# A two-layer gated transformer step on one core: first attention in four row groups, split weights of the block attention kept in DRAM, its mask added on TensorE

## The reference, cut to what matters

```python
x = x + tanh(g_xattn[0]) * first_attention(layernorm(x), ctx)   # 16 heads of 8, features = axis 1 (128), 256 positions
x = x + tanh(g_ffn[0])   * experts(layernorm(x))                # 64 routed experts and a shared one
x = x + tanh(g_xattn[1]) * mlstm(layernorm(x), ctx, ctx)        # gated linear attention
x = x + tanh(g_ffn[1])   * block(layernorm(x))                  # layernorm, causal RoPE attention (16 heads of 128), MoE
# first_attention, per batch b and head h (q, k, v are 1x1 projections of the features, with biases):
#   scores = q_h^T k_h / sqrt(128)    [256, 256], softmax over the keys, times v_h, projection by Wo
# block attention, per batch and head:
#   q, k = rope(h @ wq + bq), rope(h @ wk + bk);  scores = q k^T / sqrt(128), masked above the diagonal
#   softmax, times v, output projection wo
```

## Time and profile before

| | us |
|---|---|
| three runs | 1807.99, 1817.80, 1822.12 (median 1817.8) |
| profiled execution: time | 1817.43 |
| profiled execution: span from first to last instruction | 1816.1 |
| mean granted clock of TensorE | 0.940 of 2.4 GHz |
| busy: TensorE, VectorE, ScalarE, GpSimd | 1606.5, 1259.6, 1019.4, 765.8 |

### The profile page before, as it was taken

The page is one execution under the profiler, slowest core; times in us unless marked ns, Lnnn a source line. Parts: engine busy times, 40 slices in busy tenths (PEclk is TensorE's granted clock), DMA queues, the critical chain, the costliest instruction groups (busy, mean ns, idle before and its releaser), DMA issues.

```text
span 1816.1 us, 30483 instructions
## 1 busy us (share of the span) xinstructions
PE 1606.5 (88%) x10932; PEld 1268.4 (70%) x10932; DVE 1259.6 (69%) x2321; ACT 1019.4 (56%) x2050; POOL 765.8 (42%) x575
## 2 busy tenths in 40 slices
PE   4379999789999999999986964899899999999898
PEld 2135555368888888888872533788787778888687
DVE  6458788378644455444445576999999999999454
ACT  4247777644433335333335653877776877677453
POOL 5200000024435333333330014798798688877000
PEclk9569899899999999999996987999999999999899
DMA  5613232243343333343400002123112111211220
GB/s 155 154 55 83 76 84 61 80 111 105 94 129 106 104 110 102 108 116 102 118 10 6 4 2 92 48 72 103 56 56 68 56 56 56 68 48 30 70 47 24
DMA packets 73349, 137.42 MB, mean 76 GB/s; under 512 B 12824, under 2 KB 41308, under 8 KB 70384
## 3 DMA queue, kind: packets, MB, share of 16 engines
q1 hardware_dynamic: 73200, 135.48, 26.4%
HBM read 125.70 MB, written 8.95 MB: 74 GB/s over the span
## 4 chain that ended last, share of the span: by engine, by line
PE 54%; DVE 19%; issue 9%; DMA 8%; ACT 6%; POOL 2%; SPq 1%; DVEq 0%; ACTq 0%; POOLq 0%
PE bank L67 13%; PE bank L69 13%; PE bank L68 13%; DMA a_qs<-a_mparts 5%; DVE b_straight L1938 3%; DVE b_straight L1892 2%; PE bank L246 2%; PE bank L232 2%; PE bank L204 2%; ACT b_turned L1809 2%; DVE b_peak L1909 2%; POOL e_hidden L944 1%; DVE b_probs L1907 1%; PE bank L1700 1%; PE bank L1732 1%
## 5 line engine op out<-in xcount | busy, mean ns | idle before, releaser
L944 POOL TENSOR_TENSOR e_hidden<-e_gated,e_comb_wide 128x512 f32<-128x512 f32 x132 | 211.0, 1599 | 346.7 <-DVE e_gated L909 331.1
L784 ACT CAST e_hidden_hi<-e_hidden 128x512 fp32r<-128x512 f32 x132 | 82.0, 622 | 320.6 <-POOL e_hidden L944 320.6
L902 DVE TENSOR_TENSOR e_hidden_lo<-e_hidden,e_hidden_hi 128x512 fp32r<-128x512 f32 x132 | 98.2, 744 | 209.8 <-ACT e_hidden_hi L784 209.8
L423 DVE TENSOR_REDUCE a_negmax<-bank 128x2 f32<-128x512 f32 x256 | 165.6, 684 | 64.6 <-PE bank L204 63.3
L69 PE MATMUL bank<-e_x_hi,e_weights_lo 128*128 128x512 f32 (+1 forms) x528 | 209.5, 397 | 0.0
L67 PE MATMUL bank<-e_x_hi,e_weights_hi 128*128 128x512 f32 (+1 forms) x528 | 208.4, 395 | 0.7 <-ACT e_comb_rows L744 0.7
L68 PE MATMUL bank<-e_x_lo,e_weights_hi 128*128 128x512 f32 (+1 forms) x528 | 208.4, 395 | 0.0
L1809 ACT ACTIVATE b_turned<-bank,b_swap_bias 64x512 f32<-64x512 f32 x256 | 174.9, 683 | 17.7 <-PE bank L69 12.9
L1996 POOL TENSOR_TENSOR b_turned<-b_turned,b_rope 128x512 f32<-128x512 f32 x128 | 167.5, 1329 | 5.3 <-ACT b_turned L1809 4.8
L340 ACT ACTIVATE a_exp<-bank 128x512 f32<-128x512 f32 x256 | 142.9, 596 | 42.8 <-PE bank L232 35.4
L69 PE MATMUL bank<-e_weights_hi,e_hidden_lo 128*128 128x256 f32 (+1 forms) x528 | 149.4, 283 | 0.0
(11 more groups left out here) (326 smaller groups left out, 4318.1 us busy)
## 6 DMA issues: line engine op xcount, KB each, us to landing
e_comb_wide<-e_combT SPq DMA_DIRECT2D x130, 256.0 KB, 4.0
e_raw<-in_e_weights SPq DMA_DIRECT2D x64, 384.0 KB, 4.5
b_raw_qk<-in_b_wqk SPq DMA_DIRECT2D x64, 256.0 KB, 2.8
a_qs<-a_q_parts SPq DMA_DIRECT2D x48, 192.0 KB
a_ks<-a_k_parts SPq DMA_DIRECT2D x48, 192.0 KB
b_raw_v<-in_b_wv SPq DMA_DIRECT2D x16, 512.0 KB, 3.8
b_raw_o<-in_b_wo SPq DMA_DIRECT2D x64, 128.0 KB, 2.0
moe_comb_wide<-b_comb_rows SPq DMA_DIRECT2D x16, 256.0 KB, 6.7
```

The lines of the kernel that those rows point to most:

```text
L423: dve.tensor_reduce(m.negmax[b % 2][:, h, :], banks[h % 2][:, :].rearrange("p (q n) -> p q n", q=2), AX.X, ALU.max, negate=True).then_inc( ...
L944: pool.tensor_tensor(m.hidden[i][0:rows, :], m.gated[i][0:rows, :], m.comb_wide[u % E_RING][0:rows, chunk * BANK:(chunk + 1) * BANK], ALU. ...
```

## The change

**First attention.** q and k are split into two fp32r terms (high, low) instead of three bf16 parts. A head has 24 rows of contraction (three products of 8) and two rows for the maximum; the heads are laid out in four groups of 32 partitions (`LANES`), four heads in each. A slot `t` computes two heads: maxima for slot `t`, exponentials for slot `u = t - LEAD` (15), whose matmuls are issued in turns and lie in other row groups. Projections of the pairs of batches 2 to 7 are moved into the loop; only two pairs are projected ahead of it. One reduction takes the maxima of two heads. The maxima are split on GpSimd ahead of the turn, and two DMAs per batch carry them. Stacks are loaded per pair of batches, with a ring of three pairs. The output bias is added ahead by GpSimd, and VectorE reads the projection from the bank.

**Weights of the block attention.** During the first attention, SyncE loads 32 pieces of 512 columns of wqk, wv and wo, GpSimd rounds and subtracts, and SyncE stores both terms in DRAM. The block attention then loads both terms, with two buffers each, and neither VectorE nor GpSimd splits anything there.

**Mask.** The mask is a bf16 matmul of 512 columns with the identity, which opens the accumulation of the scores; the scale is folded into the rotation table of q. VectorE reads only the maxima; ScalarE takes the exponentials from the bank. The next mask matmul waits for the exponentials instead of for the mask addition.

```diff
-TILES = 4
-A_RING = 4
-AHEAD = HEADS + 3 * HEADS // 4
+A_TERMS, MAX_ROWS = 3, 2
+LANE, LANES = 32, 4
+A_SLOTS = HEADS // 2
+A_PAIRS = NB // 2
+A_RING, A_PARTS, A_MAXIMA, A_EXPS = 3, 2, 4, 8
+LEAD = 15
+A_LAST = NB * A_SLOTS
+A_STEPS = A_LAST + LEAD + A_SLOTS
+TURN_AT, SPLIT_EVERY = A_SLOTS + 2, 2 * A_SLOTS
...
+def projection_of(t):
+    i, at = t // SPLIT_EVERY + 2, t % SPLIT_EVERY
+    return ({0: "q", 2: "k", 4: "v"}[at], i) if at in (0, 2, 4) and i < A_PAIRS else None
...
+def heads_of(slot):
+    j = slot % A_SLOTS
+    return [(2 * (j % 2) + side, j // 2) for side in range(2)]
...
 def layer0_sp(k, m, s, ring):
+    def store(i):
+        sp.wait_ge(s.low, 2 * (i + 1))
+        both = lambda n, part: m.parts[i % A_PARTS][:, n, part, :].rearrange("p (j n) -> p j n", j=2)
+        for n, (dst, terms) in enumerate(((k.q_stack, (0, 0, 1)), (k.k_stack, (0, 1, 0)))):
+            for term, part in enumerate(terms):
+                sp.dma_start(dst[2 * i:2 * i + 2, term].rearrange("j p n -> p j n"), both(n, part).bitcast(F32)).then_inc(ring["stored"][i % A_PARTS], DMA)
+
+    def stack(i):
+        r = i % A_RING
+        sp.wait_ge(ring["stored"][i % A_PARTS], 2 * A_TERMS * DMA * (i // A_PARTS + 1))
+        if i < A_RING:
+            sp.wait_ge(s.ones, A_RING)
+        else:
+            sp.wait_ge(s.exp_scores, (i - A_RING + 1) * 2 * HEADS)
+        for src, dst in ((k.q_stack, m.qs), (k.k_stack, m.ks)):
+            for lane in range(LANES):
...
+
+    def max_rows(b):
+        sp.wait_ge(s.max_copied, b + 1)
+        for part in range(MAX_ROWS):
...
...
+    for i in range(2):
+        store(i)
+        stack(i)
+    for t in range(A_STEPS):
+        at, i = t % SPLIT_EVERY, t // SPLIT_EVERY + 2
+        if t % A_SLOTS == TURN_AT % A_SLOTS and TURN_AT <= t < A_LAST + TURN_AT:
+            b = (t - TURN_AT) // A_SLOTS
+            max_rows(b)
+            if b == 0:
+                for u in range(KEPT_SLOTS):
+                    load_kept(u)
+            else:
+                for u in kept_of(b - 1):
+                    store_kept(u)
+                for u in kept_of(b + 1):
+                    load_kept(u)
+        if at == 5 and i < A_PAIRS:
+            store(i)
+        if at == 9 and i < A_PAIRS:
+            stack(i)
...
 def layer0_pe(k, m, s, ring):
+    def scores(t):
+        u = t - LEAD
+        maximum, exponential = t < A_LAST, 0 <= u < A_LAST
+        if exponential:
+            if u % A_SLOTS == 0:
+                b = u // A_SLOTS
+                pe.wait_ge(ring["max_in"][b % A_MAXIMA], MAX_ROWS * DMA * (b // A_MAXIMA + 1))
+            if u:
+                pe.wait_ge(s.exped, 2 * u - 1)
+            exp_pair(u, 0, 0)
+        if maximum:
+            if t % (2 * A_SLOTS) == 0:
+                i = t // (2 * A_SLOTS)
+                pe.wait_ge(ring["stack_in"][i % A_RING], 2 * LANES * DMA * (i // A_RING + 1))
+            freed(("max", t))
+            max_pair(t, 0, 0)
+        if exponential:
+            exp_pair(u, 0, 1).then_inc(s.exp_scores)
+        if maximum:
+            max_pair(t, 1, 0)
+            max_pair(t, 0, 1)
+            max_pair(t, 1, 1).then_inc(s.max_scores)
+        if exponential:
+            if u:
+                pe.wait_ge(s.exped, 2 * u)
+            exp_pair(u, 1, 0)
+            exp_pair(u, 1, 1).then_inc(s.exp_scores)
...
 def layer0_pool(k, m, s, ring):
+        pool.tensor_copy(high, negmax).then_inc(own.tick())
+        pool.wait_ge(own.sem, own.n)
+        pool.tensor_tensor(low, negmax, high.bitcast(F32), ALU.subtract).then_inc(s.max_split)
+        pool.tensor_scalar(k.resid[:, b, :], k.resid[:, b, :], m.late_bias[:, 0:1], None, ALU.add).then_inc(s.biased)
+        for u in kept_of(b):
+            whole, high = kept_places(k, u, (P, KEPT))
+            pool.wait_ge(ring["kept_in"][u % KEPT_SLOTS], DMA * (u // KEPT_SLOTS + 1))
+            pool.tensor_copy(high.bitcast(F32R), whole).then_inc(s.kept_high)
+            pool.wait_ge(s.kept_high, u + 1)
+            pool.tensor_tensor(whole.bitcast(F32R), whole, high, ALU.subtract).then_inc(s.kept_low)
...
 def attention_sp(k, m, w, s, ring, before):
+    def fetch(split, whole, n, fetched):
+        for i in range(2):
+            sp.dma_start(split[n % 2][i][:, :].bitcast(F32), whole[n % whole.shape[0], i]).then_inc(fetched[n % 2], DMA)
...
+        if 2 <= n + 1 < B_STEPS and n >= 1:
+            sp.wait_ge(s.qk_sums, 2 * n)
+            fetch(w.split_qk, k.qk_parts, n + 1, ring["qk_in"])
+        if 2 <= n - 4 < B_STEPS:
+            sp.wait_ge(s.proj_sums, n - 5)
+            fetch(w.split_o, k.o_parts, n - 4, ring["o_in"])
...
 def attention_pe(k, m, w, s, ring, before):
...
     def scores(n):
+        if n:
+            pe.wait_ge(s.exps, n)
+        else:
+            pe.wait_ge(s.constants, 2)
+        pe.matmul(banks[SC][:, :].rearrange("p (b s) -> p b s", b=CHUNK), w.ident_16[:, :], w.mask_16[:, :].unsqueeze(1).to_broadcast([P, CHUNK, S]),
+                  start=True, stop=False, skip_group_check=True)
         pe.wait_ge(s.rotated, 2 * (n + 1))
-        if n:
-            pe.wait_ge(s.masked, n)
...
 def attention_dve(k, m, w, s, ring, before):
...
-    def softmax(n):
-        dve.tensor_tensor(probs[:, :, :], by_batch(banks[SC][:, :]), w.mask[:, :].unsqueeze(1).to_broadcast([P, CHUNK, S]), ALU.add).then_inc(s.masked)
-        dve.tensor_reduce(w.peak[i][:, :], probs[:, :, :], AX.X, ALU.max, negate=True).then_inc(own.tick())
-        dve.tensor_scalar(w.peak_scaled[i][:, :], w.peak[i][:, :], SCALE, None, ALU.mult).then_inc(s.peaked)
+    def peaks(n):
+        dve.wait_ge(s.score_sums, n + 1)
+        dve.tensor_reduce(w.peak[n % 2][:, :], by_batch(banks[SC][:, :]), AX.X, ALU.max, negate=True).then_inc(s.peaked)
```

More of the change, by code:

```diff
@@ L149, in max_rows @@
-    def max_rows(b):
-        sp.wait_ge(s.max_split, b + 1)
-        for part in range(MAX_ROWS):
-            row = TERM_ROWS + part
-            sp.dma_start(m.qs[b % A_RING][row:row + 1, :, :].rearrange("o h (q n) -> o (h q) n", q=2),
-                         m.mparts[b % 2][:, part, :]).then_inc(ring["max_in"][b % A_RING], DMA)
-    for i in range(1, NB // 2 + 1):
-        store_parts(i - 1)
-        if i == 3:
-            stack(0)
-    for b in range(1, A_RING):
-        stack(b)
-    for i in range(AHEAD):
-        if i >= 2 and (i - 2) % HEADS == HEADS - 1:
-            max_rows((i - 2) // HEADS)
@@ L223, in exponentials @@
-    def exponentials(b, h):
-        bank, r, at = banks[2 + h % 2], b % A_RING, b * HEADS + h
-        if h == 0:
-            pe.wait_ge(ring["max_in"][r], MAX_ROWS * DMA * (b // A_RING + 1))
-        if at >= 2:
-            pe.wait_ge(s.exped, at - 1)
-        else:
-            pe.wait_ge(s.v_copied, NB // 2)
-        for kb in range(2):
-            last = pe.matmul(bank[:, kb * POS:(kb + 1) * POS], m.ks[r][0:ROWS, h, kb * P:(kb + 1) * P], m.qs[r][0:ROWS, h, :],
-                             start=True, stop=True)
-        last.then_inc(s.exp_scores)
@@ new lines, in times_v @@
+    def times_v(g):
+        b, h = divmod(g, GROUPS)
+        pe.wait_ge(s.exped, TILES * (g + 1))
+        pe.wait_ge(s.max_copied, min((g + 3) // GROUPS + 1, NB))
+        if g:
+            pe.wait_ge(s.sums_copied, g)
+        else:
+            pe.wait_ge(s.cleared, 1)
+        for kb in range(2):
+            for lane in range(LANES):
+                last = pe.matmul(banks[SUM_BANK][LANE * lane:LANE * lane + HD + 1, 0:POS], m.vaug[:, b, kb, GROUPS * lane + h, :],
+                                 m.expo[(TILES * g + lane) % A_EXPS][:, kb, :], start=kb == 0, stop=kb == 1)
+        last.then_inc(s.weighted)
@@ L343, in times_v @@
[L343 to L369 removed]
+    for i in range(2):
+        for kind in "qk":
+            high(kind, i)
@@ new lines, in layer0_act @@
+    for chunk in range(1, NCHUNK):
+        root(chunk)
+    act.wait_ge(k.gates_in, DMA)
+    act.activation(k.gates[:, :], k.gates[:, :], ACT.Tanh).then_inc(k.gates_ready)
+    for t in range(A_STEPS):
+        u = t - LEAD
+        if t and projection_of(t - 1) and projection_of(t - 1)[0] in "qk":
+            high(*projection_of(t - 1))
+        if 0 <= u < A_LAST:
+            exponentials(u)
+        if t % A_SLOTS == TURN_AT % A_SLOTS and TURN_AT <= t < A_LAST + TURN_AT:
+            max_to_rows((t - TURN_AT) // A_SLOTS)
+        if u % 2 == 0 and 2 <= u < A_LAST + 2:
+            times_v((u - 2) // 2)
+        if u % A_SLOTS == 4 and u >= 12:
+            to_features(u // A_SLOTS - 1)
@@ new lines, in layer0_dve @@
+    norm_start(0)
+    dve.memset(m.vaug[:, :, :, :, HD], 1.0)
+    dve.memset(banks[SUM_BANK][:, :], 0.0).then_inc(s.cleared)
+    norm_end(0)
+    for kind, i in USES[:4]:
+        read(kind, i)
+    for chunk in range(1, NCHUNK):
+        norm_start(chunk)
+        if chunk == 1:
+            for i in range(2):
+                read("v", i)
+    for chunk in range(1, NCHUNK):
+        norm_end(chunk)
+    dve.wait_ge(s.weights_in, 5 * DMA)
```

(15 more changed lines are left out.)

588 lines of the change are left out of this document (245 added, 343 removed).

## The result

The changed kernel takes 1869.2 us (median, 1867.18 to 1874.99) against 1816.02 of the kernel before on the same chip: ratio 1.030, 95% interval 1.025 to 1.035. It is slower; 1786 was predicted. The profiled run took 1867.18 us, its span is 1865.8.

The account below looks back on a forecast made before the run. TensorE was taken to bound the first attention's main part, VectorE and TensorE closely the block attention. First attention 4, block 26 and its start 1 us gained: 1817.4 - 4 - 26 - 1 = 1786.4 us, range 1754 to 1832.

Parts of the forecast that it names:

- Start: First attention's start: first maximum at 37 us, first exponential at 70 instead of 110.93, 41 us gained.
- Five waits: First attention: TensorE waits five times for the maxima's DMA behind stack loads in SyncE's list, 11 us each, 55 in all.
- Slots: First attention's main part: 113 slots with maxima and exponentials at 3.44 us per four heads, 194 us, bounds 181 to 230.
- 2.0 "without a wait": Sign of being wrong, first attention: a slot costs over 2.0 us without a wait.
- a clock of 1.00 between the waits: Sign expected in the first attention: TensorE's granted clock is 1.00 between the five waits.
- the row groups don't run side by side: Rival, first attention: weight loads follow each other, 1.0 us a head, 32 us more, total 1818; chance 0.19.
- The low clock: Rival, first attention's main part: TensorE's clock stays at 0.50, groups cost 5.5 us, 116 us more, total 1902; chance 0.05.
- no overlap with the waits at their upper bound: Slow end of the range: score matmuls in different row groups not overlapping, five waits totalling 75 us; put at 1832.
- End: First attention's last fifteen slots, only exponentials: 27.4 us, unchanged from the kernel before.
- Kept traffic: First attention: 25 MB of added traffic for rounded block attention weights is hidden, cost zero.
- Block attention: Idle time of 46 us, less 15 for the mask matmul and 5 of waits: 26 us gained, bounds 8 and 31.
- The step of 8.1 us: Sign expected in the block attention: steps of 8.1 us; steps staying at 8.8 would prove the prediction wrong.

Follow-up runs that it names:

- Number 1: Changed kernel with the stack loads issued behind the even batch's maxima in SyncE's list (index 14 instead of 9); 1797.51 us, ratio 0.983.
- number 8: Changed kernel with only VectorE's order edited: residual and quotient ahead of the slot's maxima, stack loads unmoved; 1799.26 us, ratio 0.990.
- number 6: Changed kernel with stack loads behind the maxima in SyncE's list, and VectorE's residual, reciprocal and quotient ahead of its maxima; 1734.21 us, ratio 0.953.
- number 3: Changed kernel with stack loads behind the maxima in SyncE's list and only the residual ahead of VectorE's maxima; 1774.31 us, ratio 0.972.
- number 9: Matmul bursts ahead of even batches' first exponentials: on number 8, 96 narrow 1838.91 us, six wide 1816.22; on the changed kernel, six wide 1861.71.
- numbers 7: As number 3, but only 5 of the 32 pieces of block attention weights are loaded, rounded and stored; 1767.97 us, ratio 0.972.
- number 10: Two kernels: number 6 with the mask added by VectorE, 1712.76 us; number 6's first attention without kept weights plus the old block attention, 1763.38 us.
- number 4: First attention of the kernel before with the weight rounding and storing added, block attention of the changed kernel; 1830.38 us, ratio 1.003.

## Why the prediction was wrong

**Start: right.** First maximum at 33.7 us (37), first exponential at 66.25 (70).

**Five waits: right.** 9.6 to 9.8 us each, 48.5 in all, where the prediction has 55, at the batches that it named, though 51 us apart (48 the last) and not 28; a sixth of 6.4 us lies in the start. Number 1 shows their cause, number 8 their price.

**Slots: the step that failed.** Predicted were 113 slots at "0.86 us a head", 194 us, with bounds of 181 and 230. From 66.25 us to the end of the last slot with maxima at 389.4 are 323 us, less 48.5 for the five waits 274.6: 80 too many, 1.21 us a head. That is 2.43 us a slot, 2.09 without the short waits below, past the 2.0 "without a wait" that the prediction itself names as the sign of being wrong; another of its signs, a clock of 1.00 between the waits, fails too. The term had the engines' work nearly right: number 6 takes 204.9 us for the same 113 slots, 0.91 a head, with the clock at 0.97 over them. Where no projections run beside the slots, its turns of the maxima at 201.32, 214.64 and 227.98 are 13.3 us apart, 0.83 a head. Two things were missing. One is a wait: 38 us of TensorE standing behind VectorE's 1.22 us reduction, at up to three places of a batch, where number 6 has 2 left. The prediction costed the reduction as work of VectorE, at 1.37 at most, and never asked what was queued behind it in VectorE's list. The other is the clock. Number 6's 204.9 and 36 us of waits make 241; the 34 us that are left to 274.6 go with the lower clock: 0.72 from 66 us to the end of the first attention, where number 6 has 0.99. So the 80 are 36 of waits, 34 of the clock and 10 by which the slots' own work was costed too low. That the short waits also bring the lower clock is shown by number 6: it takes only 14 us of them out of number 3, its clock over the same stretch is 0.99 instead of 0.81, and its first attention is 45 us shorter.

**The rivals.** That the row groups don't run side by side was given 0.19 and is wrong. The page "TensorE: Matmul & The Clock Gate" of the Trainium skill, "LDWEIGHTS (loading the stationary operand)", has a weight load take its columns divided by 1.2 in ns, so 107 ns for 128. By that figure eight of them in a row would be 0.86 us, an estimate; the slot's eight matmuls with their loads took 0.45 in the trace. The 3.07-fold gain for four row groups that the same page measured is not tested here: a slot has two side by side. The low clock was given 0.05 and is what happened, at less than its price: a batch at 0.50 takes 19.8 us where the rival had four groups of 5.5, and the clock is low only part of the time. Against it stood that TensorE, busiest after a gap, "brings the clock back". Behind a long wait it does, within 8 us in number 8; behind the short ones of the changed kernel it doesn't for the 14 us from 184, busy 13.90 of them, and in number 9 not for 68 us. The same page, "A second HAM failure mode: psum-queue depth-cycling", says that brief idles between groups of matmuls make the clock go up and down. Numbers 1, 3 and 6 agree with it: waits of 1.4 to 1.8 us cost 1.9 times their length, and without them the clock stays up. The page's "What's actually happening" says that activity releases the throttle. The slots behind the long waits of number 8 agree; the 68 us of number 9, at 0.50 with TensorE busy 67.54, do not.

The stated range has a slip of its own: no overlap with the waits at their upper bound is 1818 + 20 = 1838, not 1832. The measured 1869 lies outside either.

**End: 8 us long.** From 389 to 424.6 are 35.6 us instead of 27.4, at a clock of 0.78.

Together: -4 at the start, +80, -6 for the waits, +8: the first attention ends 78 us after the predicted 346.4, at 424.6. The stages between and behind give another 9.

**Kept traffic: right.** Costed at zero, and zero in numbers 7 and 10. In the first attention of before it cost 39 us (number 4). The kept weights pay only beside the new first attention; the latter pays without them (number 10).

**Block attention: right in sum.** 33 us measured, 27 predicted with its start. The step of 8.1 us is 8.04, the mask's matmul 0.23 us as costed. The wait for the exponentials is 10.0 us in all, where 5 was left. The mask on TensorE lost 19 us against VectorE doing it (number 10), so the gain is that of the other parts. What the prediction didn't draw from its own numbers is that VectorE, relieved of the rounding, had room for the mask (0.66 us of a step of 8), while TensorE had none.

**Open.** Why the clock comes back behind one gap and stays at 0.50 behind another in the same slots. Bursts of wide matmuls ended at 1.00 and bursts of narrow ones at 0.50, all fourteen and all seven, yet slots of narrow matmuls brought the clock back behind every long wait; no run makes the slots' own matmuls wide. Numbers 1 and 8 do the same work as number 6 in another order, so it is shown that without the waits the full clock stays; by which rule is not.

## What to carry to other kernels

When the bounding engine reads a bank that another engine must free, look at what stands ahead of that small operation in the other engine's list: here a reorder within one list was worth 69 us of the first attention (numbers 1 and 6). In this kernel waits of 10 us every 50 us cost 1.1 times their length, and waits of 1.4 to 1.8 us every few microseconds 1.9 times; ask of a short and frequent wait what it does to the clock. Move work to the engine that has room after the change, not before it.

## What the runs showed of the hardware

- Matmuls of 24 and 26 rows in different row groups start within 0.02 us of each other, and their weight loads of 128 four-byte columns don't add up: 0.056 us for each of the eight of a slot.
- The granted clock fell from 1.00 to 0.50 inside bursts of 96 matmuls of 24 rows with TensorE busy throughout, in six of seven, and after one of them stayed there through 68 us of slots. Bursts of six matmuls of 128 rows and 512 columns ended at 1.00 in all fourteen cases, also where they had begun at 0.50; one of these took 7.9 us.
- VectorE's maximum of 1024 elements from two PSUM banks takes 1.22 us, where two of 512 took 1.37, in every run with the new first attention, with or without GpSimd's rounding beside it.
